# Attention steps reordered by tile shape, side-by-side remainder products, doubled context tiles, scattered rows in a fused attention and mixture-of-experts kernel

## Reference, cut to what matters

```python
def block(x, ctx, g_xattn, g_ffn, Wq, Wk, Wv, Wo, bo, gate_w, fc1_w, fc1_b, fc2_w, fc2_b):
    # x (32, 128, 256), ctx (32, 128, 192), 16 heads of 64, 8 experts of width 1024, all float32
    h = layernorm(x)
    q, k, v = h @ Wq, ctx @ Wk, ctx @ Wv              # inner width 1024
    a = softmax(q k^T / 8) v                          # per batch and head
    x = x + tanh(g_xattn) * (a @ Wo + bo)
    h = layernorm(x).reshape(4096, 256)
    scores = softmax(h @ gate_w.T)                    # 8 experts
    top2, chosen = top_k(scores, 2); gates = top2 / sum(top2)
    # each expert has 1024 slots, filled by first choices in token order, then by second choices;
    # a choice that finds no slot is dropped
    per expert: relu(rows @ fc1.T + fc1_b) @ fc2 + fc2_b
    x = x + tanh(g_ffn) * (sum over both choices of gate * expert row)
    return x
```

## Time and profile before

| | |
|---|---|
| median of 3 runs | 1038.72 us (1037.49 to 1039.75) |
| profiled execution, own time | 1034.84 us |
| its span | 1033.1 us |
| attention's steady part, one group | 75.34 us |
| first layer of the first expert begins | 654.39 us |
| TensorE busy | 988.0 us (96%) |
| VectorE busy | 684.1 us (66%) |
| ScalarE busy | 478.7 us (46%) |
| GpSimd busy | 481.0 us (47%) |

### The profile page before, as it was taken

The page is one execution under the profiler, slowest core; times in us unless marked ns, Lnnn a source line. Parts: engine busy times, 40 slices in busy tenths (PEclk is TensorE's granted clock), DMA queues, the critical chain, the costliest instruction groups (busy, mean ns, idle before and its releaser), DMA issues. The chain is left out here.

```text
span 1033.1 us, 21103 instructions
## 1 busy us (share of the span) xinstructions
PE 988.0 (96%) x7314; PEld 850.9 (82%) x7314; DVE 684.1 (66%) x1607; ACT 478.7 (46%) x1502; POOL 481.0 (47%) x498
## 2 busy tenths in 40 slices
PE   6899999999999999999999997899999999999995
PEld 5678878778878878878878786799999999999995
DVE  6886895886886886886885866444455554445552
ACT  3663553553553653553553630434353544535351
POOL 7521071081180270270360244385757658585756
PEclk9999999999999999999999998999999999999998
DMA  8201110110010021011001001324436162423525
GB/s 250 83 19 44 42 59 5 39 61 20 20 61 33 7 61 41 0 61 61 0 1 62 2 1 45 130 53 116 78 98 146 44 142 41 127 56 103 126 53 66
DMA packets 49949, 63.42 MB, mean 61 GB/s; under 512 B 5977, under 2 KB 41715, under 8 KB 49907
## 3 DMA queue, kind: packets, MB, share of 16 engines
q1 hardware_dynamic: 37234, 45.41, 13.6%
q0 software_dynamic: 12672, 17.47, 10.0%
HBM read 46.45 MB, written 16.78 MB: 61 GB/s over the span
## 5 line engine op out<-in xcount | busy, mean ns | idle before, releaser
L1260 ACT ACTIVATE hid<-up,b 128x512 f32<-128x512 f32 x128 | 88.3, 690 | 84.0 <-PE up L1211 84.0
L729 ACT ACTIVATE work<-score,negmax 128x128 f32<-128x128 f32 x256 | 90.4, 379 | 79.0 <-DVE negmax L926 79.0
L729 ACT ACTIVATE probs_odd<-score,negmax 128x128 f32<-128x128 f32 x256 | 90.4, 381 | 52.1 <-DVE negmax L926 52.1
L1139 POOL DMA_INDIRECT out_dram<-eo,index_e x64 | 104.6, 1634 | 19.5 <-issue 19.2
L1312 DVE TENSOR_TENSOR eo_raw<-down,b 128x256 f32<-128x256 f32 x64 | 25.9, 425 | 124.0 <-PE down L1225 124.0
L350 POOL TENSOR_SCALAR var<-mv 128x4 f32<-128x4 f32 (+1 forms) x17 | 3.9, 227 | 216.7 <-DVE mv L781 210.5
L1305 DVE TENSOR_TENSOR hid_l<-hid,hid_h 128x512 fp32r<-128x512 f32 x128 | 88.6, 692 | 4.4
L682 ACT ACTIVATE q_sb<-proj 128x512 f32<-128x512 f32 x64 | 38.7, 604 | 104.4 <-PE proj L600 104.4
L1268 ACT ACTIVATE eo<-eo_raw,gate_e 128x256 f32<-128x256 f32 x64 | 30.9, 507 | 120.9 <-DVE eo_raw L1312 120.9
L1303 DVE CAST hid_h<-hid 128x512 fp32r<-128x512 f32 x128 | 55.1, 430 | 45.8 <-ACT hid L1260 44.0
L926 DVE TENSOR_REDUCE negmax<-score 128x4 f32<-128x512 f32 x128 | 81.8, 680 | 0.8 <-PE score L521 0.8
(11 more groups left out here) (217 smaller groups left out, 3061.8 us busy)
## 6 DMA issues: line engine op xcount, KB each, us to landing
w_raw<-fc1T_dram SPq DMA_DIRECT2D x9, 1024.0 KB, 5.4
w_raw<-fc_dram SPq DMA_DIRECT2D x9, 1024.0 KB, 9.8
rows<-x_dram SPq DMA_DIRECT2D x16, 512.0 KB, 4.1
out_dram<-rows SPq DMA_DIRECT2D x8, 512.0 KB, 2.8
xn_rows<-rows SPq DMA_DIRECT2D x8, 512.0 KB, 2.8
c_raw<-ctxT_dram SPq DMA_DIRECT2D x8, 256.0 KB, 3.7
c_raw<-ctxT_dram SPq DMA_DIRECT2D x16, 128.0 KB, 4.4
b<-fc2b_dram SPq DMA_DIRECT2D x9, 128.0 KB, 9.0
```

The source lines that it names most:

```text
L729: last = nc.scalar.activation(probs[j % 2][:, c, :], score[hh][:, b * P:(b + 1) * P], ACT.Exp, bias=negmax[:, j % 2, c:c + 1], accum_out=s ...
L1139: pool.indirect_dma_start(out=out_rows[:, :], out_offset=bass.IndirectOffsetOnAxis(ap=index_e[par][:, half * GB + i:half * GB + i + 1], ax ...
L1260: nc.scalar.activation(hid[m % 2][:, :], up[m % 2][:, :], ACT.Relu, bias=b1[par][:, m:m + 1]).then_inc(s_hid, 1)
```

## The change

1. TensorE's step is ordered by the tile shape of the matmuls: transposes of the probabilities (now two steps behind), Q, K of the *next* step, V, the extra work, all with full tiles; then the last matmuls of K and V, then the scores, which use 64-row tiles; then the weighed values, which use 64-column tiles.
2. The last matmul of K and the last of V now use only 64 rows each: K's the rows 0 to 63, V's the rows 64 to 127. They stand one behind the other (`keys_rest`, `values_rest`).
3. Each kind of product has its own PSUM bank (`key_bank`, `value_bank`, `query_bank`, `out_bank`); `av` has one bank instead of two, `pT` one buffer instead of two, `k_sb` two instead of one.
4. The context tiles are doubled, K and V read the same ones, and a group's context is split one group ahead (`split_ctx`); there is no copy for K.
5. Tokens are not found through a table. Each normalised row is packed with its token number and its unnormalised gate, and GpSimd scatters it to the slots of both of its choices (`dispatch`, 8 indirect DMAs a group) in a DRAM tensor `disp`, which is first filled with blank rows by one DMA (8192 rows of 1032 bytes). The one-hot tiles and the products T0, T1 are gone. In the experts phase SyncE loads the rows with plain DMAs and VectorE reads token and gate from them (`meta`).
6. ScalarE takes the exponentials of step u-1 in step u, ahead of Q's copy; VectorE evicts V at the end of its step, behind the extra work. The extra work moves to steps 2 (O0, O1), 4 (XA, XB), 5 (LG), 6 (PR) and 7 (FA, FB, slots).
7. In `finish` VectorE instead of GpSimd computes the low halves of the first expert's weights, and the order changes with it. Warming matmuls are placed differently: 40 behind PR, none between the transposes and the logits, and not the 26 ahead of the first rows.
8. All hardware loops are written out.

```diff
+MISC = {2: ["O0", "O1"], 4: ["XA", "XB"], 5: ["LG"], 6: ["PR"]}
+def misc_of(u):
+    g, j = divmod(u, NP)
+    if j == NP - 1:
+        return ["FA", "FB"] if g < NG - 1 else []
+    return MISC.get(j, []) if g > 0 else []
...
-    xn2_dram = nc.dram_tensor("xn2_rows", [N + PAD, D], f32, kind="Internal").ap()
+    disp = nc.dram_tensor("disp", [E * CAP, W], f32, kind="Internal").ap()
...
-    cv_h, cv_l, cv_d = (sb(n, [P, TOK], f32r) for n in ("cv_h", "cv_l", "cv_d"))
-    ck_h, ck_l, ck_d = (sb(n, [P, TOK], f32r) for n in ("ck_h", "ck_l", "ck_d"))
+    c_h, c_l, c_d, c_t = ([sb(f"{n}{par}", [P, TOK], f32r) for par in range(2)] for n in ("c_h", "c_l", "c_d", "c_t"))
...
-    proj = [ps("proj0"), ps("proj1")]
+    key_bank, value_bank, query_bank, out_bank = ps("key_bank"), ps("value_bank"), ps("query_bank"), ps("out_bank")
     score = [ps("score0"), ps("score1")]
     probT = [ps("probT0"), ps("probT1")]
-    av = [ps("av0"), ps("av1")]
...
+            if g < NG - 2:
+                sp.wait_ge(s_c_ready, g + 2)
+                load_ctx(g + 2)
...
+        sp.wait_ge(s_blank, 1)
+        sp.dma_start(disp.rearrange("(t p) w -> p t w", p=P),
+                     blank[:, :].unsqueeze(1).to_broadcast([P, E * CAP // P, W])).then_inc(s_blank_out, 16)
...
+        def dispatch(g):
...
+            for j in range(2):
+                for b in range(GB):
+                    pool.indirect_dma_start(
+                        out=disp[:, :], out_offset=bass.IndirectOffsetOnAxis(ap=slots[:, j, b:b + 1], axis=0),
+                        in_=packed[:, b, :], in_offset=None,
+                        bounds_check=E * CAP - 1, oob_is_err=False).then_inc(s_disp, 16)
...
+            else:
+                split_ctx(1)
+            if g < NG - 2:
+                pool.wait_ge(s_k_ready, NP * (g + 1))
+                split_ctx(g + 2)
+            if has_prev:
+                dispatch(g)
+            dispatched(g)
...
+        def keys_rest(i):
+            g, j = divmod(i, NP)
+            c = slice(j * P, (j + 1) * P)
+            mm(key_bank[:, :], wk_e[0:R2, c], c_d[g % 2][0:R2, :], start=False, stop=True).then_inc(s_k_ready, 1)
...
+        def values_rest(bank, i):
...
+            mm(bank[:, :], c_t[g % 2][R2:P, keys], wv_e[R2:P, cols], start=False, stop=True).then_inc(s_v_ready, 1)
...
+        def step(u):
+            kinds, w, i = misc_of(u), u - 2, u + V_AHEAD
+            if w >= 0:
+                transpose_probs(w)
+            query(u)
+            if u == 0:
+                keys_main(0)
+                keys_rest(0)
+                pe.wait_ge(s_v_done, 1)
+                values_main(value_bank, i)
+                keys_main(1)
+            else:
+                if u + 1 < STEPS:
+                    keys_main(u + 1)
+                if i < STEPS:
+                    pe.wait_ge(s_v_done, i)
+                    values_main(value_bank, i)
+            if kinds:
+                pe.wait_ge(s_q_done, u + 1)
+                misc(kinds[0], query_bank, u // NP)
+            if kinds[1:]:
+                pe.wait_ge(s_at_split, w)
+                misc(kinds[1], out_bank, u // NP)
+            if u + 1 < STEPS:
+                keys_rest(u + 1)
+            if i < STEPS:
+                values_rest(value_bank, i)
+            scores(u)
+            if w >= 0:
+                if kinds[1:]:
+                    pe.wait_ge(*misc_done(kinds[1], u // NP))
+                else:
+                    pe.wait_ge(s_at_split, w)
+                weigh_values(w)
         def wait_warm(count):
-            keep_warm(nc, av[1], wk_h[:, 0:P], wk_h[:, 0:TOK], count)
+            keep_warm(nc, key_bank, wk_h[:, 0:P], wk_h[:, 0:TOK], count)
...
+        def step(u):
+            g, kinds = u // NP, misc_of(u)
+            if u > 0:
+                exponentials(u - 1, 0)
+            if u > 2:
+                attention_high(u - 3)
+            if u > 0:
+                exponentials(u - 1, 1)
+            act.wait_ge(s_q_ready, u + 1)
+            high(q_sb[:, :], query_bank[:, :], SCALE).then_inc(s_q_done, 1)
+            if "XA" in kinds:
+                act.wait_ge(s_xt_ready, 2 * g - 1)
+                high(xn2T[:, 0, :], query_bank[:, :]).then_inc(s_xa_done, 1)
+            if "PR" in kinds:
+                act.wait_ge(s_gdiff, g)
+                nc.scalar.activation(packed[:, :, D + 1], gdiff[:, :], ACT.Exp).then_inc(s_gexp, 1)
+            if "FA" in kinds:
+                for k in range(DK):
+                    act.wait_ge(s_f_ready, 2 * g + 3 + k)
+                    high(xT_h[:, k, :], (query_bank, out_bank)[k][:, :]).then_inc(s_f_hi, 1)
+            if u == 0:
+                keys_out(0)
+            if u + 1 < STEPS:
+                keys_out(u + 1)
...
+        def step(u):
+            g, j = divmod(u, NP)
+            has_prev, has_next = g > 0, g < NG - 1
+            if u > 0:
+                maxima(u - 1)
+            if u > 1:
+                probs_out(u - 2)
+            if u > 0:
+                scale_probs(u - 1, 0)
+            if u > 2:
+                attention_low(u - 3)
+            if u > 0:
+                scale_probs(u - 1, 1)
+            if has_next and j == 0:
+                dve.wait_ge(s_x_in, 16 * g + 32)
+                row_stats(xn, stats1, (0, 1))
+            if has_next and j == 1:
+                whole_stats(row_stats(xn, stats1, (2, 3)), stats1, mv1, s_stats1)
+            if has_next and j == 2:
+                dve.wait_ge(s_rstd1, g + 2)
+                normalise(xn, xn, mv1, rstd1, s_xn_ready)
+            if has_next and j == NP - 1:
+                for k in range(DK):
+                    dve.wait_ge(s_f_hi, 2 * g + 3 + k)
+                    low(xT_l[:, k, :], (query_bank, out_bank)[k][:, :], xT_h[:, k, :]).then_inc(s_f_split, 1)
+            if has_prev and j == 2:
+                residual_start(g)
+                residual(g, query_bank, 0)
+                whole_stats(residual(g, out_bank, 1), stats2, mv2, s_stats2)
+            if has_prev and j == 3:
+                dve.wait_ge(s_rstd2, g)
+                dve.wait_ge(s_disp_done, g)
+                normalise(xn2, x1, mv2, rstd2, s_xn2_ready)
+            if has_prev and j == 4:
+                dve.wait_ge(s_xt_ready, 2 * g)
+                V.tensor_copy(xn2T[:, 1, :], out_bank[:, :]).then_inc(s_xb_done, 1)
+            if has_prev and j == 5:
+                dve.wait_ge(s_lg_ready, g)
+                V.tensor_copy(logits[:, :, :], query_bank[:, 0:GB * E].rearrange("p (b e) -> p b e", b=GB)).then_inc(
+                    s_lg_done, 1)
+                dve.wait_ge(s_lg_done, g)
+                route_masks(g)
+            if has_prev and j == 6:
+                dve.wait_ge(s_pr_ready, g)
+                V.tensor_copy(ranks[:, :], query_bank[:, 0:4 * GB * E]).then_inc(s_pr_done, 1)
+                route_counts(g)
+            if has_prev and j == 7:
+                route_slots(g)
+            if u + V_AHEAD < STEPS:
+                values_out(u + V_AHEAD)
...
+            dve.wait_ge(s_e0_hi, 2)
+            low(wo_l[:, :, :], w2_raw[:, :, :], wo_h[:, :, :]).then_inc(s_e0_lo, 1)
+            dve.wait_ge(s_first_done, 1)
...
+        def load_rows(e, half):
+            src = disp_v[bass.ds(e, 1), half * TOK:(half + 1) * TOK, :]
+            sp.dma_start(rows[half][:, :, :], src.rearrange("o (i p) w -> p (o i) w", p=P)).then_inc(rows_in[half], 16)
...
+        def meta(n, e, half):
+            dve.wait_ge(rows_in[half], 16 * (e + 1))
+            if not (isinstance(e, int) and e == 0):
+                dve.wait_ge(scatters[half], 16 * GB * e)
+                dve.wait_ge(s_eo_ready, GB * n - GB)
+            weight = rows[half][:, :, D + 1]
+            me.enter(3 * n)
+            V.tensor_copy(index[half][:, :], rows[half][:, :, D])
+            i = me.mark(V.tensor_scalar(den[:, :], weight, 1.0, None, ALU.add))
+            i = me.mark(V.tensor_tensor(share[:, :], weight, first[:, bass.ds(e, 1), half * GB:(half + 1) * GB].rearrange(
+                "p o h -> p (o h)"), ALU.max))
+            me.after(i)
+            i = me.mark(V.reciprocal(den[:, :], den[:, :]))
+            me.after(i)
+            V.scalar_tensor_tensor(out=gate[half][:, :], in0=share[:, :], scalar=tanh_g[:, 1:2], in1=den[:, :],
+                                   op0=ALU.mult, op1=ALU.mult).then_inc(s_meta, 1)
```

805 lines of the change are left out of this document (296 added, 509 removed).

## The result

| | before | after |
|---|---|---|
| median of 5 runs, us | 1038.72 (1037.18 to 1039.75) | 1054.59 (1053.03 to 1058.69) |
| span of the profiled execution, us | 1033.1 | 1056.9 |
| last scores start, us | 596.01 | 620.45 |
| first layer of the experts starts, us | 654.39 | 679.99 |

After to before is 1.0161 (95% interval 1.0145 to 1.0177): 1.6% slower, clear of the noise, though less than 2%. The forecast was 1024, faster. Measured again in three later sets, the unedited kernel took 1042.84, 1041.01 and 1042.43 us, ratios 1.0055 (1.0031 to 1.0079), 1.0020 (0.9989 to 1.0052) and 1.0040 (1.0015 to 1.0066), and its runs spread from 1034.7 to 1050.0, those of before in the same sets only from 1035.0 to 1041.7. So it is not faster in any set; how much slower it is, 1.6% or the 0.2 to 0.6% of the later sets (once not to be told from nothing), changes from set to set.

The account below looks back on a forecast made before the run. TensorE was taken to set the time. Terms -18.5 - 2 + 1 + 7 - 2.3 = -14.8 took the profiled 1034.84 us to 1020.0; the median lies 3.9 above, so 1024, range 1008 to 1042.

Parts of the forecast that it names:

- first eight steps: Start of attention: steps gain 0.2 us each and lose a wait of about 0.4, -2 us.
- the loop, with the fill's +1: Eighth to last scores: groups fall from 75.34 to 72.6 us, -18.5 over 6.84 groups; filling `disp` adds +1.
- between the phases: Last scores to first expert layer: 8 indirect DMAs at 1.6 us each lengthen it, +7 us net (+2 to +12).
- B: Slower: V's eviction holds up the maxima far more, GpSimd and VectorE blocking; 6 us a group, 1046; chance 0.14.
- The step on TensorE: Plain attention step falls from 7.0 to 6.8 us through paired half matmuls and one change of shape fewer.
- the pair: Last half matmuls of K and V run side by side, 0.30 us instead of 0.46: 0.16 saved a step.
- the order by shape: One of four changes of tile shape in a step goes: 0.04 us saved.
- Rival A: The two halves run one after the other and the new shape drains: 1040, no change; chance 0.1.
- Table products and V's wait: T0 and T1 go, 2.5 us a group; V's wait for its shared bank goes, 1.1, plus 0.3 for shorter waits.
- VectorE's lateness: Maxima late after extra work and V's eviction in steps 2, 5 and 7 stall TensorE, 2.8 us a group.
- The fill: Filling `disp` at about 390 GB/s takes 22 us; x for the third group comes 1 us late, +1.
- Rival C: The fill of `disp` takes twice as long: 1044; chance 0.08.

Follow-up runs that it names:

- the first set: Four edits of the changed kernel: no scatter in the loop 1021.45 us, scatter in step 2 1024.49, head's order 1021.74, V's copy behind the maxima 1004.06.
- the best version: Changed kernel with V's copy moved, head reordered, fill halved, loop scatter in landed pairs, half in next step 2, slots in step 0: 988.45 us, 0.9511.
- one edit: Changed kernel with V's copy behind the maxima, head reordered, fill in halves and slots in the next group's step 0: 1013.06 us, 0.9761.

## Why the prediction was wrong

| part | forecast | profile |
|---|---|---|
| first eight steps | -2 | +7.0 (87.91 for 80.92) |
| the loop, with the fill's +1 | -17.5 | +17.4 (532.5 for 515.1) |
| between the phases | +7 | +1.2 (59.5 for 58.4) |
| experts and end | -2.3 | -1.8 (376.9 for 378.7) |
| sum | -14.8 | +23.8 |

**The step that failed** is one that the prediction did not take: it priced the scatter's 8 indirect DMAs between the phases alone and put them at nothing inside the loop, without a reason. There they make TensorE's signals late. The only set that has both kernels puts this at 16.7 us; the three repeats lie 17 to 20 above the loop without the scatter, and the first profile 532.5 - 498.3 = 34, across two sets. Of the 38.6 us between forecast and profile, the loop has 34.9 and the first eight steps 9.0. No rival had the signals; B, the slower one, laid its price on VectorE and GpSimd. What is shown is that the burst is needed for it and that pacing the burst takes it away. What made it absent in the first set, with the same burst, stays open. The four profiles of that set are also the only ones of the changed kernel and its edits in which the trace lost no signal's record.

**The step on TensorE** was right in kind and too small: 6.57, not 6.8, from 7.04. From the query's first matmul to the scores it takes 3.72 us (69.82 to 73.54), for 3.90 before (61.57 to 65.47): the pair, with the change of shape ahead of it, gives 0.18, forecast 0.16. From the scores to the query it takes 2.85, for 3.14: the order by shape gives 0.29, forecast 0.04. That term was mis-sized; it is read from these lines, and no run changes the order alone. Rival A is out: the halves start 0.01 us apart, and the step is shorter, not longer.

**Table products and V's wait** are gone: the changed kernel's page has no such line, and in its loop no matmul of V waits for its bank.

**VectorE's lateness** was right in place and near in size. Forecast were 0.4 us ahead of step 3's scores, 0.35 in step 4, 0.6 in step 6 and 1.5 ahead of step 0's. When V's copy was moved, the scores of steps 3, 4 and 6 gained 0.39, 0.54 and 0.60, and those of step 0 0.6, and 1.2 with the slots moved as well. Not foreseen were 0.5 us in step 7, behind step 6's counts. V's place measures 2.35 us a group and the slots' 0.8: 3.2, forecast 2.8.

**A group without late signals** takes 72.1 to 72.8 us, forecast 72.6. That is in part luck. The eight steps saved 8 x 0.47 = 3.8 us and not 1.6, and VectorE's lateness cost 0.4 more than forecast; by these alone the group should have come to 70.8. The rest was lost in the steps with extra work: beyond eight plain steps a group took 75.34 - 8 x 7.04 = 19.0 before and 68.97 - 8 x 6.57 = 16.4 in the best version, which has next to no lateness left, so 2.6 less where the forecast took off 2.5 + 1.4. In the same way the kernel without the scatter comes to 1021.3 to 1021.5 us, close to 1024, with errors of both signs in it.

**The first eight steps** (-2, measured +7.0). The prediction followed VectorE's waits within a running group, not in the first one, where GpSimd still splits weights. With the new order on GpSimd the ninth scores come at 80.11 (80.92 before, 87.91 in the changed kernel), with V's copy moved as well at 77.7 to 78.4.

**The fill**: 34.5 us for a forecast of 22, as its rate was taken from loads. It costs (8.81 + 19.56) - (6.57 + 17.46) = 4.3 us, not 1. Rival C was right in half of its size and priced five times too high.

**Between the phases** the sum was +7 and the profile shows +1.2. Every indirect DMA was priced at 1.6 and took 1.27, the residual began 19.7 us after the last scores, not 21.4, and from the slots (657.98) to the first layer it took 22.0 us, not 26.2. The sum's lower bound is given as +2, but 1.36 for each of the two scatters' DMAs makes it 7 - 2 x 8 x 0.24 = 3.2.

## What to carry to other kernels

Work that goes to an idle engine's DMA queue is not free for the others: look, after the change, for waits whose releaser had ended long before, and bound how many indirect DMAs are under way; two to four at a time cost nothing in this loop, but 14 and 5 us where the scatter stood alone between the phases. When an operation is put at the end of an in-order engine's step, whatever that engine waits for is passed on through it; follow this in the first iterations too, where other engines still do one-off work. And price a chain of matmuls by the distances between each two kinds that follow one another.

## What the runs showed of the hardware

TensorE's signals reached ScalarE and VectorE up to 4.7 us late (5.1 in one edit) beside the fourth to eighth of a burst of indirect DMAs of 128 rows of 1032 bytes, 1.28 us apart, while VectorE's and ScalarE's own were never more than 0.03 us late. Beside four at a time they were up to 1.8 us late, beside two up to 1.3, and in the kernels without them in the loop 0.2 at most. The expert phase's four scatters with addition and the gathers before them, 1.64 and 1.06 us each, showed nothing of it. In one set of four kernels, three of which issued the burst, it was absent altogether, which stays open; so does what in the chip is shared.

Matmuls of 512 columns on full tiles start 0.23 us apart, one of half the rows 0.33 behind a full one, a full one 0.43 behind a half, and two halves in different rows 0.01 apart. A fill of 1032-byte rows from one SBUF tile ran at 245 GB/s where loads ran at 390, and x, issued behind it at 73.1, took 15 us to land where that page's median is 5.1. In a stretch of 8 us TensorE was busy 3.45, and for the next 4 us of full work its granted clock was 0.50, 1.2 GHz.
